# Inverse roots of a two-layer transformer kernel as one power instruction on GpSimd

## The chip, the cores and the metric

The kernel runs on one core of a Trainium2 chip. A core has TensorE (PE in the profile, its weight loads as PEld), VectorE (DVE), ScalarE (ACT), GpSimd (POOL) and SyncE (SP, which issues most DMAs), each with its own instruction stream; they meet by semaphores. The metric is the device time of one execution in microseconds, the median of three runs.

## The reference, cut to what matters

The input `x` is 8 x 256 tokens of 512 features, taken as 2048 tokens; the context is as many tokens of 256 features.

```python
def layernorm(x):  return (x - mean(x)) / sqrt(var(x) + 1e-5)
def rmsnorm(q, g): return q * rsqrt(mean(q*q) + 1e-5) * g      # over the 128 of a head

# first layer: cross attention (16 heads of 128, 8 key/value heads), then feed-forward
xn = layernorm(x)
q, k, v = xn @ Wq, ctx @ Wk, ctx @ Wv
x = x + softmax(q k^T / sqrt(128)) v @ Wo
x = x + feed_forward(layernorm(x))          # 512 -> 1536 -> 512, silu(gate) * up, scaled fp8 weights
# second layer: cross attention with normed queries and keys (16 heads of each), then experts
xn = layernorm(x)
q, k, v = rmsnorm(xn @ Wq, gq), rmsnorm(ctx @ Wk, gk), ctx @ Wv
x = x + softmax(q k^T / sqrt(128)) v @ Wo
x = x + experts(layernorm(x))               # 16 experts of width 256, the best 2 of sigmoid(logits)
```

An inverse root is needed four times for a layer norm (one number a token) and twice for an rms norm (one number a token and head).

## The kernel before, in words

All is in float32 precision: an operand of a product is split into a high and a low part of the faster type fp32r (`_hi`, `_lo`), and three products (high by high, high by low, low by high) make one. The tokens are 16 tiles of 128 (one a partition, `P` = 128, `NT` = 16), in four token groups of four tiles (`TG` = 4, `GT` = 512 tokens, `NG` = 4). The attention works through eight head groups of two heads (`HB` = 2, `NHG` = 8), and in each through the four token groups.

The program is five stages in a row: opening, first attention, feed-forward, second attention, experts (`moe_stage`). Each is a block in which every engine's program is written out by hand, in the order in which it is to run; a stage ends when all engines have reached its end. Work of a later stage (weights, normalised rows) is put into the stage before where room was found for it.

An inverse root is made by `rsqrt_steps` (L50): an integer seed from the bits of the number, then three Newton rounds of four small instructions. These are 13 instructions on [128, 4] or [128, 8], and each waits for the one before by a chain semaphore. They stand in these places:

- **The opening**, on VectorE: mean and variance of the first eight tiles (`bn_aggr`, then L241), the root, the shift `-mean * rstd` (L243). Then VectorE normalises tile 0, ScalarE tiles 1, 3, 5, 6 (L179) and GpSimd tiles 2, 4, 7 (L141). GpSimd's only earlier work there is the identity matrix `ident`; TensorE waits for it by `ident_made`.
- **The layer norms at the start and the end of an attention**, on GpSimd: `ln_group_factors` waits for VectorE's moments (`ln_mv`, L1379 or L1395), makes variance (L678), root and shift (L680, L683) and raises `ln_factors`. ScalarE waits for that and normalises rows (L1096), TensorE turns them (L884), and they become operands of the next stage. `late_factors(g)` does so for token group g in the last head group.
- **The second attention's rms norms**, on GpSimd: `norm_queries` waits for the sums of squares of the next token group's queries and for this group's exponentials, makes eight factors and raises `q_ready`. `norm_keys` waits for ScalarE's copy of the keys into `kn` (L1022), makes eight factors (variance L620, then the root), scales the keys by them in four instructions of 256 columns (L635) and raises `k_ready`; the first keys are scaled by VectorE instead. `first_query_factors` makes the first four query factors.
- **The last token group's layer norm before the experts**, on VectorE at the start of `moe_stage`: variance, root, shift; then VectorE normalises four rows (L2523), and ScalarE the four rows of the group before (L2390), whose factors were made in the attention.
- **The feed-forward layer's own**, on VectorE.

In each token group of the second attention VectorE takes the maxima of the scores and from them and the query factors the biases of the exponentials (L1308), ScalarE the exponentials (L1065), VectorE scales the probabilities by the reciprocal sums in pairs of instructions (L1333), TensorE turns them (L832), ScalarE and VectorE copy them out as high and low part (L1071, L1245), and TensorE multiplies them with the values (L733, as all split products). TensorE turns the scaled keys at L809. ScalarE copies the turned queries' high part at L1003 and the weighted values' high part at L1075. In `moe_stage` the routing's logits come from L2035, ScalarE's sigmoids are turned back at L2278.

`apart` raises a semaphore that nobody waits for; it separates an instruction from the wait before it.

## Time and profile before

| | |
|---|---|
| three runs | 2195.21, 2196.19 (median), 2196.66 us |
| profiled execution, span | 2195.1 us, 36404 instructions |
| TensorE (PE) busy | 2071.1 us, 94% |
| weight loads (PEld) | 1788.0 us, 81% |
| VectorE (DVE) | 1566.6 us, 71% |
| ScalarE (ACT) | 1253.3 us, 57% |
| GpSimd (POOL) | 574.9 us, 26% |

The span runs from the first to the last instruction of the profiled execution; the time of a run lies about 1 us above it. The busy shares are means over stages that differ: TensorE is at 90% or more in nearly all of the 40 slices of the page, and at about half in the first slice, in one at the change from the second attention to the experts, and in the last. A row of a timeline has the start in us, the duration of one (or the sum, where instructions of a kind stand together, x4), the engine, the line of the kernel, the operation, what it writes from what, with shapes, and in brackets how long the engine had been idle before and which instruction ended that. DVEq, POOLq and the like are an engine's sequencer.

### The profile page before, as it was taken

Reading aid. Unit: us, or ns where it says so; the run is one execution under the profiler, and the core shown is the slowest. Engines: PE = TensorE matmul, PEld = TensorE weight load, DVE = VectorE, ACT = ScalarE, POOL = GpSimd, SP = SyncE. Lnnn points to the kernel's source line nnn. Section 1 sums busy time; section 2 is a strip of 40 time slices with the busy share of each in tenths; the row PEclk is TensorE's granted clock in tenths of the full one; section 3 lists DMA queues with packets and bytes.
Section 4 is the critical chain, followed back from the end, with each engine's and each line's share of the span. In section 5 each row is a group of like instructions: output and inputs, shape, how many; then the busy total and the mean of one; then the engine's idle time right before and its main releaser. Section 6 shows DMA issues by size and latency. Waiting matters only on the chain. (4 is left out here: it accounts for less than half of the span.)

```text
span 2195.1 us, 36404 instructions
## 1 busy us (share of the span) xinstructions
PE 2071.1 (94%) x11594; PEld 1788.0 (81%) x11594; DVE 1566.6 (71%) x3714; ACT 1253.3 (57%) x3253; POOL 574.9 (26%) x1480
## 2 busy tenths in 40 slices
PE   5999999999999899999899999999999999599992
PEld 5888988888888778887788888888888887378882
DVE  6787677777779884444677777777777777767775
ACT  4555445455445533324776766677676666567771
POOL 2001001001001002223333434433343433145541
PEclk8999999999999999999999999999999999799996
DMA  7232122121211220002111111111111111278886
GB/s 249 82 99 89 63 85 92 62 89 63 90 63 49 73 77 1 1 1 77 49 58 49 62 63 57 48 57 48 57 62 72 48 40 39 87 269 290 290 275 257
DMA packets 78509, 202.10 MB, mean 92 GB/s; under 512 B 8689, under 2 KB 38409, under 8 KB 66209
## 3 DMA queue, kind: packets, MB, share of 16 engines
q1 hardware_dynamic: 68672, 179.37, 23.5%
q0 software_dynamic: 7520, 16.80, 2.2%
q10 hardware_dynamic: 2176, 4.19, 0.5%
q8 instruction: 72, 1.18, 0.2%
q14 instruction: 69, 0.56, 0.1%
HBM read 179.09 MB, written 29.10 MB: 95 GB/s over the span
## 5 line engine op out<-in xcount | busy, mean ns | idle before, releaser
L733 PE MATMUL bank<-l_wkv_hi,l_ctxT 128*128 128x512 f32 (+1 forms) x768 | 224.8, 364 | 9.0 <-PEq L79 6.9
L1245 DVE TENSOR_TENSOR l_pT_lo<-bank,l_pT_hi 128x512 fp32r<-128x512 f32 x256 | 175.2, 684 | 69.7 <-ACT l_pT_hi L1071 69.6
L1065 ACT ACTIVATE l_probs<-l_scored,l_nbias 128x256 f32<-128x256 f32 x256 | 128.4, 504 | 167.8 <-DVE l_nbias L1318 167.8
L733 PE MATMUL bank<-xnT_hi,l_wq_hi 128*128 128x512 f32 x512 | 208.7, 408 | 0.8 <-DVEq L1551 0.7
L733 PE MATMUL bank<-l_wo_hi,l_oT_hi 128*128 128x512 f32 x512 | 208.4, 407 | 0.7 <-DVE l_oT_lo L1245 0.7
L733 PE MATMUL bank<-l_wo_hi,l_oT_lo 128*128 128x512 f32 x512 | 200.6, 392 | 0.0
L733 PE MATMUL bank<-xnT_hi,l_wq_lo 128*128 128x512 f32 x512 | 200.3, 391 | 0.0
L733 PE MATMUL bank<-l_wo_lo,l_oT_hi 128*128 128x512 f32 x512 | 200.2, 391 | 0.0
L733 PE MATMUL bank<-xnT_lo,l_wq_hi 128*128 128x512 f32 x512 | 200.2, 391 | 0.0
L1071 ACT CAST l_pT_hi<-bank 128x512 fp32r<-128x512 f32 x256 | 150.8, 589 | 67.6 <-PE bank L832 67.6
L1333 DVE TENSOR_SCALAR l_probs<-l_probs,l_rden 128x256 f32<-128x256 f32 x512 | 181.3, 396 | 9.0
L1361 DVE TENSOR_TENSOR x_sb<-bank,x_sb 128x512 f32<-128x512 f32 x256 | 170.9, 683 | 7.8 <-PE bank L733 7.7
L832 PE MATMUL bank<-ident,l_probs 128*128 128x128 f32 x1024 | 156.5, 275 | 8.3 <-DVE l_probs L1333 8.3
L733 PEld LDWEIGHTS bank<-l_wkv_hi,l_ctxT 128*128 128x128 f32 x768 | 140.4, 194 | 28.9 <-issue 8.0
L1065 ACT ACTIVATE l_probs<-bank,l_nbias,l_rr 128x256 f32<-128x256 f32 x256 | 142.4, 565 | 34.2 <-DVE l_nbias L1308 33.6
L1983 PE MATMUL bank<-xnT_hi,ffn_w 128*128 128x512 f32 x384 | 151.5, 395 | 3.0 <-DVE ffn_w L1673 3.0
L733 PE MATMUL bank<-l_kT_hi,l_qT_hi 128*128 128x256 f32 x512 | 148.2, 289 | 5.7 <-DVE l_kT_lo L1245 3.1
L733 PE MATMUL bank<-l_pT_hi,l_v_hi 128*128 128x256 f32 x512 | 148.1, 289 | 5.3 <-DVE l_pT_lo L1245 4.3
L1983 PE MATMUL bank<-xnT_lo,ffn_w 128*128 128x512 f32 x384 | 149.6, 390 | 0.0
L733 PE MATMUL bank<-l_kT_lo,l_qT_hi 128*128 128x256 f32 x512 | 145.4, 284 | 0.0
L733 PE MATMUL bank<-l_kT_hi,l_qT_lo 128*128 128x256 f32 x512 | 145.4, 284 | 0.0
L733 PE MATMUL bank<-l_pT_lo,l_v_hi 128*128 128x256 f32 x512 | 145.1, 283 | 0.0
(305 smaller groups left out, 5738.0 us busy)
## 6 DMA issues: line engine op xcount, KB each, us to landing
l_ctxT<-ctx_split SPq DMA_DIRECT2D x63, 1024.0 KB, 4.8
moe_raw_gu<-in_L_ffn_gate_up_proj SPq DMA_DIRECT2D x31, 1024.0 KB
moe_raw_dn<-in_L_ffn_down_proj SPq DMA_DIRECT2D x31, 512.0 KB
l_raw_a<-in_L_xattn_Wq SPq DMA_DIRECT2D x16, 512.0 KB, 5.8
l_raw_a<-in_L_xattn_Wo SPq DMA_DIRECT2D x16, 512.0 KB, 5.6
x_sb<-in_x SPq DMA_DIRECT2D x4, 1024.0 KB, 9.1
l_v_next<-l_kn SPq DMA_DIRECT2D x16, 256.0 KB, 2.0
l_v_lo<-l_v_next SPq DMA_DIRECT2D x16, 256.0 KB, 2.6
```

What stands on the lines that cost most here:

```text
L733: mm = nc.tensor.matmul(out, a[x], b[y], start=(i == 0), stop=(i == n - 1))
L832: mm = nc.tensor.transpose(b_pt[:, S * s + P * t:S * s + P * (t + 1)], probs[u % 2][:, t, P * s:P * (s + 1)], k.ident[:, :])
L1065: ins = nc.scalar.activation(probs[u % 2][:, t, :], src, ACT.Exp, bias=nbias[:, i:i + 1], scale=scale, accum_out=rsum[:, i:i + 1])
L1071: nc.scalar.copy(pT[0][:, :, :].rearrange("p s q -> p (s q)"), b_pt[:, :]).then_inc(pT_hi, 1)
L1245: nc.vector.tensor_tensor(pair[1], src, pair[0].bitcast(F32), ALU.subtract).then_inc(done, 1)
L1333: ins = nc.vector.tensor_scalar(row, row, rden[:, 2 * u + t:2 * u + t + 1], None, ALU.mult)
L1361: nc.vector.tensor_tensor(row, b_q[t % 2][:, :], row, ALU.add).then_inc(y_added, 1)
L1983: mm = nc.tensor.matmul(out[r % 2][:, :], w[:, f, first + P * c:first + P * (c + 1)], part[:, c, at], start=(c == 0 and part is k.xnT_hi), ...
```

## The change

Outside of the feed-forward layer every inverse root becomes one GpSimd instruction, `tensor_tensor` with the power operation, of the variance and a tile `half` that holds -0.5 everywhere (`root_of`, `ROOT_STEPS` = 1). GpSimd fills `half` in the opening, ahead of the identity matrix. `rsqrt_steps` stays for the feed-forward layer.

- Opening: the root goes from VectorE to GpSimd. GpSimd waits for the variance (the chain at `CHAIN - 2`), VectorE waits for the root and makes the shift, as before.
- Attentions: GpSimd's chains are variance, power (and for a layer norm the two steps of the shift). The counts on the semaphores follow (`norm_steps`, `ln_steps`, and VectorE's waits on `k_chain` and `den_chain`).
- Experts: variance, root and shift of the last token group leave VectorE and `moe_stage`; GpSimd makes them with `late_factors(3)` at the end of its program in the second attention.

The diff, with hunks that only drop an unused scratch tile left out:

```diff
--- before.py
+++ after.py
@@ -61,6 +61,12 @@
 
 
 RSQRT_STEPS = 13
+ROOT_STEPS = 1
+
+
+def root_of(gp, y, v, half, step):
+
+    step(gp.tensor_tensor(y, v, half[:, 0:v.shape[1]], ALU.pow))
 
 
 def apart(k, eng):
@@ -92,7 +98,7 @@
         chain = k.ln0_chain
         mine = slice(0, TILES)
         DVE_TILES, ACT_TILES, POOL_TILES = (0, ), (1, 3, 5, 6), (2, 4, 7)
-        CHAIN = 2 * TILES + 1 + RSQRT_STEPS + 1
+        CHAIN = 2 * TILES + 1 + ROOT_STEPS + 1
         b_row = banks[4:8]
 
         def wait_normed(eng, t):
@@ -132,9 +138,12 @@
         def _(pool):
             gp = nc.gpsimd
             gp.memset(zero[:, :], 0.0).then_inc(ident_made, 1)
-            pool.wait_ge(ident_made, 1)
+            gp.memset(k.half[:, :], -0.5).then_inc(ident_made, 1)
+            pool.wait_ge(ident_made, 2)
             gp.affine_select(out=k.ident[:, :], in_=zero[:, :], compare_op=ALU.not_equal, fill=1.0, base=0,
                              pattern=[[-1, P]], channel_multiplier=1).then_inc(ident_made, 1)
+            pool.wait_ge(chain, CHAIN - 2)
+            gp.tensor_tensor(rstd[:, mine], var[:, mine], k.half[:, mine], ALU.pow).then_inc(chain, 1)
             pool.wait_ge(chain, CHAIN)
             for t in POOL_TILES:
                 apart(k, pool)
@@ -161,7 +170,7 @@
                     mm = nc.tensor.transpose(b_row[t % len(b_row)][:, P * c:P * (c + 1)], xn[t][:, P * c:P * (c + 1)], k.ident[:, :])
                 mm.then_inc(turned, 1)
 
-            pe.wait_ge(ident_made, 2)
+            pe.wait_ge(ident_made, 3)
             for g in range(2):
                 turn_c(g)
             for t in range(4):
@@ -239,7 +248,8 @@
             for t in range(TILES):
                 step(nc.vector.bn_aggr(mv[:, t, :], k.ln_stats[:, t, :]), t == TILES - 1)
             step(nc.vector.tensor_scalar(var[:, mine], mv[:, mine, 1], EPS, None, ALU.add))
-            rsqrt_steps(nc.vector, rstd[:, mine], tmp[:, mine], var[:, mine], step)
+            done[0] += 1
+            dve.wait_ge(chain, done[0])
             step(nc.vector.scalar_tensor_tensor(shift[:, mine], mv[:, mine, 0], -1.0, rstd[:, mine], ALU.mult, ALU.mult))
             for t in DVE_TILES:
                 nc.vector.tensor_scalar(xn[t][:, :], k.x_sb[:, t, :], mv[:, t, 0:1], rstd[:, t:t + 1],
@@ -605,7 +615,7 @@
             def weights_lo(w, raw, level, done):
                 start.weights_lo(pool, w, raw, level, done)
 
-            norm_steps = 1 + RSQRT_STEPS
+            norm_steps = 1 + ROOT_STEPS
 
             def factors(cols, chain, hg, g):
 
@@ -618,7 +628,7 @@
 
                 apart(k, pool)
                 step(gp.tensor_scalar(var[:, cols], sums[:, cols], 1.0 / HD, EPS, ALU.mult, ALU.add))
-                rsqrt_steps(gp, rr[:, cols], tmp[:, cols], var[:, cols], step, lambda: apart(k, pool))
+                root_of(gp, rr[:, cols], var[:, cols], k.half, step)
 
             def norm_keys(hg, g, first=False):
 
@@ -648,7 +658,7 @@
                 pool.wait_ge(qsum_out, 1)
                 apart(k, pool)
                 step(gp.tensor_scalar(var[:, cols], sums[:, cols], 1.0 / HD, EPS, ALU.mult, ALU.add))
-                rsqrt_steps(gp, rr[:, cols], tmp[:, cols], var[:, cols], step, lambda: apart(k, pool))
+                root_of(gp, rr[:, cols], var[:, cols], k.half, step)
 
             def norm_queries(hg, g):
 
@@ -657,14 +667,14 @@
                 factors(slice(nk, nk + nq), q_chain, hg, g - 1)
                 pool.sem_inc(q_ready, HB)
 
-            ln_steps = RSQRT_STEPS + 3
+            ln_steps = ROOT_STEPS + 3
 
             factors_before = [0]
 
             def ln_group_factors(tiles, aggregated):
 
                 at = slice(tiles[0], tiles[-1] + 1)
-                mean, var, rstd, tmp, shift = k.ln_mv[:, at, 0], *(a[:, at] for a in (k.ln_var, k.ln_rstd, k.ln_tmp, k.ln_shift))
+                mean, var, rstd, shift = k.ln_mv[:, at, 0], *(a[:, at] for a in (k.ln_var, k.ln_rstd, k.ln_shift))
                 done = [ln_steps * factors_before[0]]
                 factors_before[0] += 1
 
@@ -676,7 +686,7 @@
                 pool.wait_ge(ln_aggr, aggregated)
                 apart(k, pool)
                 step(gp.tensor_scalar(var, k.ln_mv[:, at, 1], 1.0, EPS, ALU.mult, ALU.add))
-                rsqrt_steps(gp, rstd, tmp, var, step, lambda: apart(k, pool))
+                root_of(gp, rstd, var, k.half, step)
                 step(gp.tensor_tensor(shift, mean, rstd, ALU.mult))
                 apart(k, pool)
                 step(gp.tensor_scalar(shift, shift, -1.0, 0.0, ALU.mult, ALU.add))
@@ -721,6 +731,8 @@
                         late_factors(2)
 
             iterations(pool, iteration)
+            if rms:
+                late_factors(3)
 
         @block.tensor
         def _(pe):
@@ -1380,7 +1392,7 @@
 
             def scale_first_keys():
 
-                dve.wait_ge(k_chain, 1 + RSQRT_STEPS)
+                dve.wait_ge(k_chain, 1 + ROOT_STEPS)
                 kn3 = kn[:, :, :].rearrange("p t (h d) -> p (t h) d", d=HD)
                 scale = rr[:, 0:nk].rearrange("p (a b) -> p a b", b=1).broadcast_to([P, nk, HD])
                 nc.vector.tensor_tensor(kn3, kn3, scale, ALU.mult).then_inc(k_ready, 1)
@@ -1442,7 +1454,7 @@
             if AHEAD:
                 turned_low(0, 1)
             if rms:
-                dve.wait_ge(den_chain, 1 + RSQRT_STEPS)
+                dve.wait_ge(den_chain, 1 + ROOT_STEPS)
             biases(0, 0, 0)
             if not rms:
                 denominators(0, 0, 0)
@@ -2120,8 +2132,8 @@
 
         assert nc.sbuf_base <= start.bottom
         block = st.enter_context(nc.Block())
-        factors_made, dve_normed, act_normed, turned, turned_hi, turned_lo = (
-            sem(n) for n in ("factors_made", "dve_normed", "act_normed", "turned", "turned_hi", "turned_lo"))
+        dve_normed, act_normed, turned, turned_hi, turned_lo = (
+            sem(n) for n in ("dve_normed", "act_normed", "turned", "turned_hi", "turned_lo"))
         logits_made, b_logits = start.logits_made, start.b_logits
         sigmoids_made, probs_turned, probs_copied, consts_made, route_chain, picked, ranked, rows_made, halves_made = (
             sem(n) for n in ("sigmoids_made", "probs_turned", "probs_copied", "consts_made", "route_chain", "picked", "ranked",
@@ -2515,10 +2527,6 @@
                 if wait:
                     dve.wait_ge(route_chain, done[0])
 
-            last = slice(LATE + TG, NT)
-            chain(v.tensor_scalar(var[:, last], mv[:, last, 1], EPS, None, ALU.add))
-            rsqrt_steps(v, rstd[:, last], tmp[:, last], var[:, last], chain)
-            v.scalar_tensor_tensor(shift[:, last], mv[:, last, 0], -1.0, rstd[:, last], ALU.mult, ALU.mult).then_inc(factors_made, 1)
             for t in DVE_TILES:
                 v.tensor_scalar(xn[:, t, :], k.x_sb[:, t, :], mv[:, t, 0:1], rstd[:, t:t + 1], ALU.subtract, ALU.mult).then_inc(dve_normed, 1)
             for t in range(LATE, NT):
@@ -2712,6 +2720,7 @@
         k.ln_mv = st.enter_context(nc.sbuf_tensor("ln_mv", [P, NT, 2], F32))
         k.ln_var, k.ln_rstd, k.ln_tmp, k.ln_shift = (
             st.enter_context(nc.sbuf_tensor(f"ln_{n}", [P, NT], F32)) for n in ("var", "rstd", "tmp", "shift"))
+        k.half = st.enter_context(nc.sbuf_tensor("half", [P, NT], F32))
         k.xn_stored = [k.sem(f"xn_stored{i}") for i in range(3)]
         xn_rows = nc.dram_tensor("xn_rows", (T, D), F32, kind="Internal").ap()
         rows_v = xn_rows.rearrange("(t p) d -> p t d", p=P)
```

## Rows read from the trace of the kernel before

**Rows 1.** Windows: each engine's busy us and instructions, granted clock, DMA.

```profile
1070.00:1830.00 760.00, 758.39 (x4405) 661.68 (x4405) 557.55 (x1203) 524.28 (x1644) 301.49 (x1045) 1.00 0.15 54
```

**Rows 2.** Timeline, opening: start us, us, engine, line, idle before and its releaser.

```profile
12.98 0.17 DVE L241 TENSOR_SCALAR ln_var<-ln_mv 128x8 f32<-128x8 f32 x1
...
15.83 0.17 DVE L243 SCALAR_TENSOR_TENSOR ln_shift<-ln_mv,ln_rstd 128x8 f32<-128x8 f32 x1
...
16.23 2.52 POOL L141 TENSOR_SCALAR xn<-x_sb,ln_rstd,ln_shift 128x512 f32<-128x512 f32 x3 [14.68 <-DVE ln_shift L243]
...
17.08 1.52 ACT L179 ACTIVATE xn<-x_sb,ln_shift,ln_rstd 128x512 f32<-128x512 f32 x2
```

**Rows 3.** Timeline, first attention's start: GpSimd, ScalarE, TensorE.

```profile
37.55 0.20 POOL L678 TENSOR_SCALAR ln_var<-ln_mv 128x8 f32<-128x8 f32 x1 [7.99 <-DVE ln_mv L1395]
...
37.95 0.20 POOL L54 TENSOR_SCALAR ln_rstd<-ln_var 128x8 int32<-128x8 int32 x1 [0.20 <-POOL ln_var L678]
...
41.94 0.20 POOL L680 TENSOR_TENSOR ln_shift<-ln_mv,ln_rstd 128x8 f32<-128x8 f32 x1
...
42.62 1.52 ACT L1096 ACTIVATE ffn_raw<-x_sb,ln_shift,ln_rstd 128x512 f32<-128x512 f32 x2 [3.44 <-POOLq L683]
...
44.04 0.56 ACT L1003 CAST l_qT_hi<-bank 128x512 fp32r<-128x512 f32 x1
...
43.48 1.36 PE L884 MATMUL bank<-ident,ffn_raw 128*128 128x128 f32 x8 [0.85 <-ACT ffn_raw L1096]
```

**Rows 4.** Timeline, first attention's end: GpSimd, ScalarE, VectorE, TensorE.

```profile
717.85 0.19 POOL L678 TENSOR_SCALAR ln_var<-ln_mv 128x4 f32<-128x4 f32 x1 [13.46 <-DVE ln_mv L1379]
...
724.17 1.52 ACT L1096 ACTIVATE l_raw_a<-x_sb,ln_shift,ln_rstd 128x512 f32<-128x512 f32 x2 [4.23 <-POOLq L683]
...
726.19 0.69 DVE L1245 TENSOR_TENSOR l_oT_lo<-bank,l_oT_hi 128x512 fp32r<-128x512 f32 x1 [1.73 <-ACT l_oT_hi L1075]
...
727.62 0.36 PE L733 MATMUL bank<-l_pT_hi,l_v_hi 128*128 128x256 f32 x1 [1.89 <-DVE l_pT_lo L1245]
```

**Rows 5.** Timeline, second attention's loop: groups from 1506 and 1532, one instruction at 1581.

```profile
1515.93 0.40 ACT L1022 COPY l_kn<-bank 128x256 f32<-128x256 f32 x1
...
1517.32 0.20 POOL L620 TENSOR_SCALAR l_var<-l_sums 128x8 f32<-128x8 f32 x1 [0.36 <-POOL l_rr L60]
...
1521.72 2.38 POOL L635 TENSOR_TENSOR l_kn<-l_kn,l_rr 128x256 f32<-128x256 f32 x4
...
1517.41 0.16 DVE L1308 SCALAR_TENSOR_TENSOR l_nbias<-l_mx,l_rr 128x2 f32<-128x2 f32 x1
...
1519.04 0.62 DVE L1333 TENSOR_SCALAR l_probs<-l_probs,l_rden 128x256 f32<-128x256 f32 x2
...
1523.12 1.13 DVE L1333 TENSOR_SCALAR l_probs<-l_probs,l_rden 128x256 f32<-128x256 f32 x2
...
1581.29 0.53 DVE L1308 SCALAR_TENSOR_TENSOR l_nbias<-l_mx,l_rr 128x2 f32<-128x2 f32 x1
...
1520.30 0.60 PE L832 MATMUL bank<-ident,l_probs 128*128 128x128 f32 x4
...
1524.31 0.42 PEld L832 LDWEIGHTS bank<-ident,l_probs 128*128 128x128 f32 x4 [0.15 <-DVE l_probs L1333]
...
1550.08 0.42 PEld L832 LDWEIGHTS bank<-ident,l_probs 128*128 128x128 f32 x4 [0.43 <-DVE l_probs L1333]
```

**Rows 6.** Timeline, from the second attention to the routing.

```profile
1871.16 0.38 DVE L1379 BATCH_NORM_AGGREGATE ln_mv<-ln_stats 128x2 f32<-128x6 f32 x4
...
1877.53 1.91 DVE L2523 TENSOR_SCALAR moe_xn<-x_sb,ln_mv,ln_rstd 128x512 f32<-128x512 f32 x4
...
1872.83 0.39 PE L2035 MATMUL bank<-xnT_lo,moe_gwT_hi 128*16 128x512 f32 x1
...
1873.53 2.93 ACT L2390 ACTIVATE moe_xn<-x_sb,ln_shift,ln_rstd 128x512 f32<-128x512 f32 x4 [11.42 <-PEq L386]
...
1880.42 0.61 PE L2278 MATMUL bank<-ident,moe_probT 16*128 16x16 f32 x4 [3.25 <-ACT moe_probT L2399]
```

More of the change, by code:

```diff
@@ L83, in opening_stage @@
         xn = [st.enter_context(nc.sbuf_tensor(f"xn_{j}", [P, D], F32)) for j in range(TILES)]
-        mv, var, rstd, tmp, shift = k.ln_mv, k.ln_var, k.ln_rstd, k.ln_tmp, k.ln_shift
+        mv, var, rstd, shift = k.ln_mv, k.ln_var, k.ln_rstd, k.ln_shift
         block = st.enter_context(nc.Block())
@@ L408, in attention_stage @@
             nk, nq = TG * nkv, TG * HB
-            sums, var, rr, tmp = (sb(n, [P, nk + nq]) for n in ("sums", "var", "rr", "tmp"))
+            sums, var, rr = (sb(n, [P, nk + nq]) for n in ("sums", "var", "rr"))
             gain_in = sb("gain_in", [P, 2])
@@ L2093, in moe_stage @@
         token_of, dest_of, expert_of = sb("token_of", [P, HALVES], I32), sb("dest_of", [P, HALVES], I32), sb("expert_of", [P, 2 * PAIRS], I32)
-        mv, var, rstd, tmp, shift = k.ln_mv, k.ln_var, k.ln_rstd, k.ln_tmp, k.ln_shift
+        mv, rstd, shift = k.ln_mv, k.ln_rstd, k.ln_shift
         warm = sb("warm", [P, 2])
```

## The prediction, before the changed kernel was run

> **What bounds the kernel now.** I read the windows first, to see which engine is full in which stretch, then the timelines of single stretches, looking for places where an engine stands idle behind an inverse root. In the second attention's loop TensorE is busy 758.4 of 760 us while VectorE has 558, ScalarE 524 and GpSimd 301 [rows 1]: shortening a GpSimd chain there is worth something only where it takes a stall away from TensorE. The start of each stage is different: there the engines hand work to each other and a root can set the pace. So I went to each of the places where a root is made.
>
> **The price of one root.** The old chain is 13 instructions: a seed and three rounds of four. A small instruction of GpSimd runs 0.20 us. A whole layer norm group (variance, 13 steps, two for the shift) goes from 37.55 to 42.62, when ScalarE takes over: 5.07 us. The seed starts at 37.95 and the shift at 41.94 [rows 3], so the 13 steps are 3.91 with the 0.08 between instructions off. After the change the same group is 5.07 - 3.91 = 1.16 us + X, where X is the power instruction.
>
> No row shows X. From below it is a multiply of the same shape, 0.20 us. From above it is the chain it replaces, 3.9 us. Between them: the key scaling, 128x256 in 0.595 us (four in 2.38 [rows 5]) against 0.20 for 8 columns, gives (0.595 - 0.20) / 248 = 1.6 ns a column. If a logarithm and an exponential are each worth one old chain, 26 arithmetic steps, X is 0.20 + 26 x 8 x 1.6 ns = 0.53 us for 8 columns and 0.37 for 4. Loops that don't fill the pipeline make it longer. I take 0.65 and 0.43 us, nearer to the lower end because the multiply's row shows that most of a small instruction is fixed cost. If the lanes were served one after another it would be 0.20 + 16 x 0.33 = 5.5 us.
>
> **Opening.** The variance ends at 13.15, the shift starts at 15.83 [rows 2]. Now the root crosses to GpSimd and back: a crossing is 0.23 (16.00 to 16.23), the way back some 0.1, so the shift starts at 13.15 + 0.23 + X + 0.1 = 14.1. That is 1.7 us earlier and worth nothing: the reader is to see that ScalarE starts to normalise at 17.08, with no idle time named, because it is still copying the context; the shift was there at 16.00. ScalarE is what the rest of this stage hangs on. The cover is 1.0 us; only with X above 2.7 does the root come too late. The extra memset of `half` lies beside a wait of 14.7 us [rows 2]. I book 0.
>
> **First attention, start.** ScalarE idles 3.44 us for the factors and normalises from 42.62; after it comes the copy of the second head's queries, at 44.04. TensorE had finished that product at 43.48 - 0.85 = 42.63 [rows 3]. With the factors at 37.55 + 1.16 + 0.65 = 39.4, two rows are normalised by 40.9 and the copy starts at 42.7, held by TensorE. Everything up to the first scores hangs on that copy: 44.04 - 42.71 = **-1.3 us**, in full for X up to 2.5.
>
> **First attention, end.** The late group starts at 717.85; ScalarE idles 4.23 us until 724.17, so it was free at 719.94. Behind that wait stand the copy of the weighted values and of the turned probabilities; VectorE waits 1.73 for them until 726.19, TensorE 1.89 until 727.62 [rows 4]. With the factors at 717.85 + 1.16 + 0.43 = 719.4 ScalarE goes on at once, its two copies end by 722.6, and VectorE goes on when it is done with its own work, at 726.19 - 1.73 = 724.46. TensorE's 1.89 falls to about 0.1: **-1.8 us**, in full for X up to 3.
>
> **Second attention, start.** Three chains in a row (keys, first queries, layer norm). VectorE is busy with statistics when the keys' factors come, TensorE's first scores come after the queries' factors, ScalarE's normalisation stands behind its own copies. Nobody waits for GpSimd there; 0.
>
> **Second attention, loop.** Of the 32 groups (8 head groups by 4 token groups) all but the first have their keys scaled by GpSimd: 31 groups each lose two chains of 3.9 us on an engine that nobody waits for. Yet there is an indirect effect. The reader is to look at the pair of probability scalings L1333: 0.62 us at 1519.04, but 1.13 at 1523.12 [rows 5]. The slow one lies under GpSimd's key scaling, 1521.72 to 1524.10, and ends 0.15 after it. TensorE waits for it: its weight load at 1524.31 carries 0.15 idle, and every fourth group it is 0.43, as at 1550.08 [rows 5]. TensorE is the bound, so that is lost time; with an estimated 0.07 by which the load before it is already late I count 0.22 in an ordinary group and 0.50 in each fourth.
> With one power instruction the key scaling moves. The keys' last copy ends at 1516.33; + 0.2 crossing + 0.28 variance = 1516.81, + X + 0.08: it runs 1517.54 to 1519.92. It now meets the scaling before, at 1519.04. Waiting first for the third and then for the fourth GpSimd instruction, that pair ends at 1519.92 + 0.16 = 1520.08 in place of 1519.66, 0.42 late. TensorE wants it at 1520.30 less its load [rows 5]: just hidden. VectorE carries the 0.42 on: the next pair starts at 1523.54, takes 0.62 free of GpSimd, and the load can go at 1524.22 where it went at 1524.31; in each fourth group at 1549.71 where it was 1550.08. That saves 0.09 in 22 groups and 0.37 in 8 (the first group has another order): 2.0 + 3.0 = **-5.0 us**. If the lateness were hidden wholly it would be 22 x 0.22 + 8 x 0.50 = -8.8.
>
> **Second attention's end and the routing.** ScalarE's wait before normalising late rows ends nothing that TensorE waits for. The last group's moments end at 1871.54 [rows 6]. After the change GpSimd makes their factors there: start 1871.7, + 1.1 + X = 1873.2. TensorE's last product ends at 1873.22 anyway, and the next stage starts at 1873.53. So no cost at X = 0.43, and X - 0.45 above it. What is gained is 4.0 us of VectorE, which now normalises from 1873.5 and not from 1877.53. That is not on the path: TensorE waits 3.25 us until 1880.42 for ScalarE's sigmoids [rows 6], which stand behind ScalarE's own four rows from 1873.53. 0.
>
> **The sum.** 0 - 1.3 - 1.8 + 0 - 5.0 + 0 = -8.1 us on a span of 2195.1: 2187.0. The three runs have their median at 2196.19, 1.1 above the span; with it 2188.1.
>
> **Rivals.**
> *Only the ends gain.* The lateness that the key scaling now causes one pair earlier eats what it no longer causes: 2196.2 - 3.1 = 2193. For it: by the same sums the saving per ordinary group is 0.09 us, and it is gone at X = 0.78. Against: each fourth group has more to give back.
> *The power instruction keeps VectorE off.* This ends on the other side. L1308 at 1517.41 reads two tensors of SBUF; at 1581.29 such a one took 0.53 in place of 0.16 [rows 5], with GpSimd at a weight split. The power instruction runs from 1516.81: with X above 0.6 it is in flight at 1517.41. At X = 1.5 L1308 ends at 1518.41 in place of 1517.57, the exponentials and the pair follow, the pair then meets the key scaling's last instruction and ends at 1520.9, TensorE stands 0.8 us less the 0.2 that it lost before, in all some 0.7 x 31 = 22 us, - 2 for the fourth groups, - 3 at the ends: 2213. It decides from X = 0.78 on, with 3 us for each further 0.1; from X about 0.95 the kernel is slower. Against it: at 1517.41 GpSimd's variance (1517.32 to 1517.52) is in flight, too, and L1308 takes its plain 0.16.
> The Trainium skill, SBUF — State Buffer, "Who interferes with whom", says of a VectorE instruction with two SBUF inputs, or in a two-port mode, that whichever engine issues first holds the shared pair for its whole instruction and the other blocks. By that rule this rival's arithmetic holds wherever X is above 0.6; the late pair at 1523.12 agrees with it, the plain 0.16 at 1517.41 does not show it.
> *A very slow power instruction.* With lanes in turn, 5.5 us, TensorE would stand some 5 us in each of 31 groups: 2340.
> The Trainium skill, GPSIMD Engine Reference, "Instruction dispatch", has about 6 us for the first call of newly loaded code. By it the opening's shift would come at 20 and not at 14, some 3 us behind ScalarE's readiness. No first instruction of a kind in this trace shows such a gap.
>
> **How the numbers follow.** A measurement of this kernel tells about 0.2% from no change, 4.4 us: faster is below 2191.8, slower above 2200.6. X up to 0.78, or a longer one that doesn't hold VectorE: 0.50, 2184 to 2191.8, faster. Only the ends gain, X of 0.78 to 0.95 or a collision as dear as before: 0.20, mostly within 0.2%. Keeping VectorE off: 0.23, slower. Very slow, or dear code loading: 0.07, slower. So 0.50, 0.20, 0.30. The likeliest case is 2188.1, its own range 2184 to 2192. For 8 in 10 the upper end reaches into the second rival to X about 1.3, 2196.2 - 5 + 17 = 2208; the lower end is the loop's stalls gone wholly, 2196.2 - 3.1 - 8.8 = 2184.
>
> **What would show it.** After: one GpSimd instruction of 0.4 to 0.7 us where 13 were; the first attention's scores 1.3 us earlier; no idle of ScalarE at its late rows; in the loop the key scaling under the third pair of L1333 and not the fourth, and the period of four groups some 0.6 us shorter; the routing starting as far behind TensorE's last product as now. Wrong: a root longer than 0.78 us, L1308 at more than 0.16 with the root in flight, or the third pair ending after 1520.2 on this scale, so that TensorE waits there.

## The result and the profile after

The changed kernel takes 2202.89 us (median of 5 runs, 2201.36 to 2203.88), the kernel before 2195.21 (5 runs, 2194.02 to 2196.66): ratio 1.0033, 95% interval 1.0022 to 1.0045. It is slower by some 7 us, where I had forecast 8 less. The profiled execution has a span of 2199.4 us.

The new instruction first. GpSimd's groups by line and shape (count, busy us, mean ns, idle time before):

```profile
L69 POOL TENSOR_TENSOR l_rr<-l_var,half 128x8 f32<-128x8 f32 x64 | 104.7, 1637 | 5.3
...
L69 POOL TENSOR_TENSOR ln_rstd<-ln_var,half 128x4 f32<-128x4 f32 x7 | 7.1, 1007 | 0.6
```

X is 1.64 us for 8 columns and 1.01 for 4: 0.158 us for each column and 0.38 beside. I had taken 0.65 and 0.43. It is still less than half of the chain's 3.9.

The timeline of the second attention's loop, the group that answers to [rows 5] (2.4 us later in this execution):

```profile
1518.93 0.20 POOL L630 TENSOR_SCALAR l_var<-l_sums 128x8 f32<-128x8 f32 x1 [1.94 <-ACT l_kn L1034]
1519.21 1.64 POOL L69 TENSOR_TENSOR l_rr<-l_var,half 128x8 f32<-128x8 f32 x1
1520.92 2.42 POOL L645 TENSOR_TENSOR l_kn<-l_kn,l_rr 128x256 f32<-128x256 f32 x4
...
1519.82 0.16 DVE L1320 SCALAR_TENSOR_TENSOR l_nbias<-l_mx,l_rr 128x2 f32<-128x2 f32 x1
...
1521.45 1.42 DVE L1345 TENSOR_SCALAR l_probs<-l_probs,l_rden 128x256 f32<-128x256 f32 x2
...
1526.17 0.61 DVE L1345 TENSOR_SCALAR l_probs<-l_probs,l_rden 128x256 f32<-128x256 f32 x2
...
1522.93 0.42 PEld L844 LDWEIGHTS bank<-ident,l_probs 128*128 128x128 f32 x4 [0.29 <-DVE l_probs L1345]
1526.84 0.42 PEld L844 LDWEIGHTS bank<-ident,l_probs 128*128 128x128 f32 x4
```

And the third pair's load in the kernel before:

```profile
1520.19 0.46 PEld L832 LDWEIGHTS bank<-ident,l_probs 128*128 128x128 f32 x4
```

The reader is to see three things. The key scaling (L645) has moved from the fourth pair of probability scalings to the third, as forecast. But it lies over the whole third pair, which takes 1.42 us in place of 0.62, and TensorE's load at 1522.93 waits 0.29 us for it, where the one at 1520.19 in the kernel before did not wait. And the bias (L1320, 0.16 us) is not touched by the power instruction, which is in flight from 1519.21 to 1520.85.

The first attention's start and end, and the way into the routing:

```profile
36.31 1.64 POOL L69 TENSOR_TENSOR ln_rstd<-ln_var,half 128x8 f32<-128x8 f32 x1
...
38.72 1.52 ACT L1108 ACTIVATE ffn_raw<-x_sb,ln_shift,ln_rstd 128x512 f32<-128x512 f32 x2 [1.16 <-POOLq L693]
...
41.16 0.58 ACT L1015 CAST l_qT_hi<-bank 128x512 fp32r<-128x512 f32 x1 [0.91 <-PE bank L745]
...
716.67 1.01 POOL L69 TENSOR_TENSOR ln_rstd<-ln_var,half 128x4 f32<-128x4 f32 x1
...
718.97 1.52 ACT L1108 ACTIVATE l_raw_a<-x_sb,ln_shift,ln_rstd 128x512 f32<-128x512 f32 x2 [0.51 <-POOLq L693]
...
724.29 0.19 PEld L745 LDWEIGHTS bank<-l_pT_hi,l_v_hi 128*128 128x128 f32 x1 [0.26 <-issue]
...
1876.58 0.39 PE L2047 MATMUL bank<-xnT_lo,moe_gwT_hi 128*16 128x512 f32 x1
...
1877.27 0.19 POOL L692 TENSOR_SCALAR ln_shift<-ln_shift 128x4 f32<-128x4 f32 x1 [0.20 <-POOL ln_shift L690]
...
1877.89 2.93 ACT L2402 ACTIVATE moe_xn<-x_sb,ln_shift,ln_rstd 128x512 f32<-128x512 f32 x4 [12.00 <-PEq L396]
...
1884.78 0.42 PE L2290 MATMUL bank<-ident,moe_probT 16*128 16x16 f32 x4 [3.25 <-ACT moe_probT L2411]
```

ScalarE waits 0.51 us where it waited 4.23 [rows 4], the queries' copy is held by TensorE and no more by the factors, and from ScalarE's first row of the routing to the turned probabilities it is 6.89 us as before [rows 6]. But that first row starts 0.92 us after TensorE's last product (1876.97 to 1877.89), where it was 0.31 (1873.22 to 1873.53): the last factors, ready at 1877.46, now come after that product.

What no row of mine had shown is in a stage whose code did not change. The groups of the feed-forward layer's products, changed kernel (mean ns last before the idle time):

```profile
L1995 PE MATMUL bank<-xnT_hi,ffn_w 128*128 128x512 f32 x384 | 153.3, 399 | 1.9 <-DVE ffn_w L1685 0.8
L1995 PE MATMUL bank<-xnT_lo,ffn_w 128*128 128x512 f32 x384 | 151.6, 395 | 0.0
```

Before they were 395 and 390 ns. Matmuls overlap, so their starts tell more: followed one by one in the two traces, such products (`xnT_hi` with `ffn_w`, then `xnT_lo` with `ffn_w`) start 227.5 ns apart before and 233.2 after, at the same granted clock of 1.00. That is the mean of the gaps below 260 ns; a longer one holds a stall. The forecasts below have 227.8 for the same. Where a stretch is bounded by TensorE that is time. I matched the weight loads of both traces by their number (11594 in each): the 1152 of the feed-forward layer's middle take 3.8 us longer after the change, 3632 of the first attention's loop 2.4 us longer. The same counting gives the period of the second attention's loop, four token groups: 102.13 us before, 102.68 after. These two numbers, stretch and period, are the measures of what follows.

### The profile page after: what moved, and what is told of

The parts are those of the page before. It is cut to its first block and busy times, and to the rows that moved or that the text cites. A ratio compares the mean times of both kernels' runs of the same rounds, so it can differ in the third digit from the quotient of the medians.

```text
span 2199.4 us, 34874 instructions
## 1 busy us (share of the span) xinstructions
PE 2075.8 (94%) x11594; PEld 1780.7 (81%) x11594; DVE 1565.1 (71%) x3686; ACT 1260.5 (57%) x3253; POOL 502.9 (23%) x622
## 5 line engine op out<-in xcount | busy, mean ns | idle before, releaser
L1345 DVE TENSOR_SCALAR l_probs<-l_probs,l_rden 128x256 f32<-128x256 f32 x512 | 188.1, 409 | 9.0
L1015 ACT CAST l_qT_hi<-bank 128x512 fp32r<-128x512 f32 x128 | 75.1, 587 | 127.2 <-PE bank L745 125.1
L745 PE MATMUL bank<-l_pT_hi,l_v_lo 128*128 128x256 f32 x512 | 144.9, 283 | 0.0
```

The source lines that it names most:

```text
L745: mm = nc.tensor.matmul(out, a[x], b[y], start=(i == 0), stop=(i == n - 1))
L1015: nc.scalar.copy(qT[h][0][:, :], b_q[h][:, :]).then_inc(q_hi, 1)
L1345: ins = nc.vector.tensor_scalar(row, row, rden[:, 2 * u + t:2 * u + t + 1], None, ALU.mult)
```

## The experiments

Theory 1: the tile `half` (64 bytes a partition) has pushed all tiles behind it to other addresses, and that slows TensorE. Theory 2: in the second attention the collision of the key scaling with the third pair costs more than the old one with the fourth. The rival to the first is that the pace differs by chance from one execution to another; to the second, that the power instruction keeps VectorE off.

**A tile that nobody uses.**

```diff
 # kernel before
+        k.pad = st.enter_context(nc.sbuf_tensor("pad", [P, NT], F32))   # where the change has half
```

> The kernel before, with one unused tile of 16 columns (64 bytes a partition) laid where the change lays its tile of -0.5, so that all tiles behind it lie 64 bytes further. Theory 1 (placement): in the changed kernel the products of 128x512 follow each other at 0.232 us in the feed-forward layer and 0.2317 in the first attention, where they stood at 0.227 and 0.2297 before, though their code is the same; the shift does it. Then this kernel shows the same slower pace, the feed-forward layer is 4 us longer, the first attention 2.4, and the whole is slower by 5 to 8 us (ratio 1.002 to 1.004). Rival: the pace differs from one execution to another and has nothing to do with the change; then this kernel takes the time of before within 2 us (ratio 0.999 to 1.001).

Ratio 1.0044 (1.0030 to 1.0058), feed-forward stretch +3.8 us, first attention +2.3: an unused tile does to the kernel before all that the change does to these two stages, and the whole becomes 9.7 us longer, more than by the change (7.2), with intervals that overlap. In the second attention's loop it does little: period 102.17.

**Every tile back in its place.**

```diff
 # changed kernel: half takes the scratch tile's place
-        k.ln_var, k.ln_rstd, k.ln_tmp, k.ln_shift = (... ("var", "rstd", "tmp", "shift"))
-        k.half = st.enter_context(nc.sbuf_tensor("half", [P, NT], F32))
+        k.ln_var, k.ln_rstd, k.half, k.ln_shift = (... ("ln_var", "ln_rstd", "half", "ln_shift"))
+        k.ln_tmp = k.ln_shift
-            sums, var, rr = (... ("sums", "var", "rr"))
+            sums, var, rr, _ = (... ("sums", "var", "rr", "spare"))
```

> The changed kernel, with the tile of -0.5 in the place of the scratch tile that the roots no longer need (the feed-forward layer's own root takes the shift's tile as scratch) and the second attention's scratch tile kept as an unused one, so that every other tile lies where it lay before. Placement theory: the pace goes back to 0.227 in the feed-forward layer, and the time falls from 2202.9 by 2.4 + 3.9 + about 1 to 2195.6 (ratio to before 1.000). Rival, pace by chance: as the changed kernel, ratio 1.003.

Ratio 0.9986 (0.9977 to 0.9995), 2192.73 us: faster than before, where I had expected equality. Stretch -0.05 us. Placement cost the change 0.0047 of 2196 us, 10.3 us, more than the 7.3 that I had added up from three stages. The period is 102.36, and 102.68 in the changed kernel: the loop has 2.5 us of it (7.75 periods), though the unused tile alone cost it next to nothing.

**The key scaling held back.**

```diff
 # changed kernel, norm_keys
+                apart(k, pool)
+                pool.wait_ge(p_normed, count(UN, 3, hg, g))
                 for i in range(0, nk, PIECE // HD):
```

> The changed kernel, with GpSimd's key scaling in the second attention made to wait until VectorE has scaled the third pair of probabilities. Collision theory: the third pair takes 0.62 us in place of 1.42, TensorE's turning load waits no longer (gap 0.48 to about 0.14), the fourth pair stays free; 31 groups save 0.34 each, 10 us: ratio to before 0.9985. Rival: the stall is not of this collision, or the scaling, 1.3 us later, meets the fourth pair or makes the turned keys late; then ratio 1.002 to 1.006.

Ratio 0.9985 (0.9976 to 0.9994), period 101.47: 1.21 us less than the changed kernel's. Timeline of this kernel, GpSimd and VectorE:

```profile
1515.37 0.62 DVE L1347 TENSOR_SCALAR l_probs<-l_probs,l_rden 128x256 f32<-128x256 f32 x2
1516.06 2.33 POOL L647 TENSOR_TENSOR l_kn<-l_kn,l_rr 128x256 f32<-128x256 f32 x4 [1.30 <-DVE l_probs L1347]
1517.21 0.62 DVE L1322 SCALAR_TENSOR_TENSOR l_nbias<-l_mx,l_rr 128x2 f32<-128x2 f32 x1
1519.74 0.62 DVE L1347 TENSOR_SCALAR l_probs<-l_probs,l_rden 128x256 f32<-128x256 f32 x2
```

The scaling fits between the two pairs, and both take 0.62 us. It now lies over a bias instead, which takes 0.62 us and not 0.16, and the period falls all the same. An engine that nobody waits for was made to start later, and the kernel became faster by 10 us.

**The old chain in the loop alone.**

```diff
 # changed kernel, factors() only (norm_steps, the wait on k_chain and the scratch tile with it)
-                root_of(gp, rr[:, cols], var[:, cols], k.half, step)
+                rsqrt_steps(gp, rr[:, cols], tmp[:, cols], var[:, cols], step, lambda: apart(k, pool))
```

> The changed kernel, with the old chain of 13 instructions for the factors of keys and queries in the second attention's loop alone (layer norms and first query factors keep the power instruction). Collision theory: the loop shows the pattern of before (fourth pair slow, third free), 0.19 us less in an ordinary group and 0.09 more in each fourth: 3.7 us off, ratio to before 1.0016. Rival, the loop is not what costs: ratio stays at 1.003.

Ratio 1.0023 (1.0014 to 1.0032), period 102.43, not 102.13: the direction is as forecast, the size some 2 us in place of 3.7. The unused tile alone gave a period of 102.17, so 0.26 us of it is not explained.

**Shifts by 128 and 32 bytes.**

```diff
 # kernel before, two runs
+        k.pad = st.enter_context(nc.sbuf_tensor("pad", [P, 2 * NT], F32))   # 128 bytes; [P, NT // 2] for 32
```

> The kernel before with one unused tile of 128 bytes a partition in the place where the earlier run had 64. Theory: what slows the products is that their operands no longer begin at a multiple of 128 bytes (the feed-forward weights begin at 116096 = 907 x 128, with the 64 byte tile at 116160). Then a shift by 128 costs nothing: feed-forward stretch as before, ratio 0.999 to 1.001. Rival: any shift against the tiles ahead (the turned activations stay where they are) costs the same: ratio 1.003 to 1.005, feed-forward +3.8 us.

> The same with 32 bytes. If 128 byte lines count, an operand that begins in the middle of one costs the same whether it is off by 32 or by 64: feed-forward stretch +3.8 us, ratio 1.003 to 1.005. If 32 bytes were the step that counts (all tiles still begin at multiples of 32), ratio 1.000, but then the 64 byte tile should have cost nothing either.

128 bytes: ratio 1.0031 (1.0020 to 1.0042), stretch +3.5. 32 bytes: 1.0052 (1.0038 to 1.0066), stretch +3.9. My theory of 128-byte lines fell: a shift by a whole line costs nearly the same. These two shifts also cost where the 64 bytes did little: the loop's period is 102.40 with 32 bytes and 102.38 with 128, and the experts' products from 1930 to 2150 us take 2.7 and 1.7 us longer (0.6 with 64). But the pace by pairs of operands pointed on. Mean ns between the starts of products of 512 columns, gaps below 260 ns (the last column is the next experiment):

| product, then the next | before | +32 B | +64 B | +128 B | 64 B ahead of all |
|---|---|---|---|---|---|
| xnT_hi with ffn_w, then xnT_lo with ffn_w | 227.5 | 232.5 | 233.3 | 235.7 | 227.6 |
| xnT_lo with ffn_w, then xnT_hi with ffn_w | 227.5 | 234.0 | 233.3 | 229.9 | 227.6 |
| xnT_hi with l_wq_hi, then xnT_lo with l_wq_hi | 229.3 | 233.3 | 233.5 | 232.2 | 230.6 |
| moe_w_dn_lo with xnT_hi, then moe_w_dn_hi with xnT_lo | 226.7 | 234.6 | 231.2 | 232.1 | 226.7 |
| l_wo_hi with l_oT_hi, then l_wo_lo with l_oT_hi | 228.4 | 228.1 | 227.3 | 228.1 | 230.1 |
| ffn_w with ffn_fz_hi, then ffn_w with ffn_fz_lo | 226.8 | 228.8 | 229.1 | 229.2 | 226.8 |
| ffn_w with ffn_fz_lo, then ffn_w with ffn_fz_hi | 226.8 | 230.1 | 231.1 | 229.6 | 226.8 |

In the first four rows one operand moved (weights) and one did not (`xnT`, laid ahead of the new tile), and all are slower. In the last three both moved. The row of `l_wo` is no slower behind `xnT` (with the tile ahead of all it is, by 1.7 ns); those of `ffn_w` with `ffn_fz` are, by 2.0 to 4.3 ns.

**The same tile ahead of all others.**

```diff
 # kernel before
+        k.pad = st.enter_context(nc.sbuf_tensor("pad", [P, NT], F32))
         k.x_sb = st.enter_context(nc.sbuf_tensor("x_sb", [P, NT, D], F32))
```

> The kernel before with the unused 64 bytes ahead of all tiles, so that the turned activations move as well and every tile lies to every other as before, except for the few that are counted from the end of the memory. The runs so far show a slower pace where a product takes one operand that moved and one that did not (turned activations with feed-forward or query weights: 227.8 to 233.3 ns), with shifts of 32, 64 and 128 bytes. Theory, the distance between the two operands counts: these products stay at 227.8 and the feed-forward stretch as long as before, ratio 0.999 to 1.001. Rival, the address of the moving operand itself counts: 233, feed-forward stretch +3.8 us, ratio 1.003 or more.

Ratio 1.0002 (0.9993 to 1.0011), stretch -0.03 us, period 102.15. The same shift of 64 bytes costs nothing when `xnT` takes part in it. So it is not a tile's own place that counts, but how the tiles that moved lie to those that stayed. That it is the distance between a product's own two operands is not shown: `ffn_w` and `ffn_fz` moved together behind `xnT` and got slower, and move together here and do not. The groups of these products, first with the tile ahead of all, then (second fence) behind `xnT`:

```profile
L1983 PE MATMUL bank<-xnT_hi,ffn_w 128*128 128x512 f32 x384 | 151.6, 395 | 2.9 <-DVE ffn_w L1673 2.9
L1983 PE MATMUL bank<-xnT_lo,ffn_w 128*128 128x512 f32 x384 | 149.6, 390 | 0.0
```

```profile
L1983 PE MATMUL bank<-xnT_hi,ffn_w 128*128 128x512 f32 x384 | 153.3, 399 | 1.8 <-DVE ffn_w L1673 0.8
L1983 PE MATMUL bank<-xnT_lo,ffn_w 128*128 128x512 f32 x384 | 151.6, 395 | 0.0
```

**The layer norms alone.** Every tile in its place, and the old chain in the loop.

> The changed kernel with every tile where it lay before, and the old chain of 13 instructions for the factors of keys and queries in the second attention's loop: what is left of the change are the layer norms (opening, attention starts and ends, the routing's last group). By my prediction's terms the ends give 3.1 us; the loop then has the period of before, 102.14 us for four groups, where the unshifted power version has 102.36, so it is some 1.7 us faster than that one: ratio 0.998. Rival: the loop's period differs for another reason than the chains; then it stays at 102.36 and the ratio at 0.9986.

Ratio 0.9981 (0.9972 to 0.9990), period 102.21. The layer norms by one instruction give 4.2 us, and some 4.8 if the loop's 0.08 a period over the kernel before is set aside. The loop itself, with the power instruction and no shift, has 102.36: 0.15 more a period, 1.2 us over its 7.75 periods, and 0.23 or 1.8 us more than in the kernel before. The two ratios (0.9986 and 0.9981) say 1.1, less than their intervals can tell; the period rests on one trace each.

**Both repairs.**

> Both repairs together: every tile where it lay before, and the key scaling held back until the third pair is scaled. If the two costs are separate, they add: the period falls from 102.36 by the 1.2 us that the hold-back gave in the shifted kernel to 101.15, and the time to 2192.7 - 9.3 = 2183.4, ratio 0.994. Rival: they overlap (a stall hides behind a slower pace), then 0.996 to 0.9985.

Ratio 0.9943 (0.9929 to 0.9957), 2184.36 us, period 101.19. The two costs are separate and add up within the intervals: the hold-back gives 1.21 a period with the shift and 1.17 without.

**More work, less time.**

```diff
 # changed kernel, tiles in their places, factors()
+                if chain is k_chain:
+                    gp.tensor_tensor(spare[:, cols], var[:, cols], k.half[:, 0:nk], ALU.pow)
                 root_of(gp, rr[:, cols], var[:, cols], k.half, step)
```

> The changed kernel with every tile where it lay before, and the power instruction for the keys' factors issued twice (once into an unused tile), so that this step takes GpSimd 3.3 us and not 1.6. Collision theory: the key scaling then begins 1.7 us later, after the third pair of probabilities and before the fourth, and more work makes the kernel faster: period of four groups 101.2 us in place of 102.36, ratio 0.9943 as with the hold-back. If the power instruction itself kept VectorE off, its second copy would cost: the small bias instruction takes more than 0.16 us and the period is above 102.4, ratio above 0.9986.

Ratio 0.9940 (0.9927 to 0.9954), period 101.19. Its timeline:

```profile
1506.48 1.64 POOL L632 TENSOR_TENSOR l_spare<-l_var,half 128x8 f32<-128x8 f32 x1
1508.08 1.64 POOL L69 TENSOR_TENSOR l_rr<-l_var,half 128x8 f32<-128x8 f32 x1
1509.79 2.33 POOL L647 TENSOR_TENSOR l_kn<-l_kn,l_rr 128x256 f32<-128x256 f32 x4
...
1507.10 0.16 DVE L1322 SCALAR_TENSOR_TENSOR l_nbias<-l_mx,l_rr 128x2 f32<-128x2 f32 x1
...
1508.73 0.62 DVE L1347 TENSOR_SCALAR l_probs<-l_probs,l_rden 128x256 f32<-128x256 f32 x2
...
1510.57 0.42 DVE L1322 SCALAR_TENSOR_TENSOR l_nbias<-l_mx,l_rr 128x2 f32<-128x2 f32 x1
```

A power instruction that is thrown away makes the kernel 10 us faster (0.9940 and 0.9986) than the same without it, since the key scaling starts after the third pair. The pair at 1508.73 lies wholly under a power instruction and takes its plain 0.62; the bias takes 0.16 under the power instruction and 0.42 under the key scaling. It holds in the whole loop: each of the 31 biases that start under a power instruction takes 0.16, and each of the 62 instructions of such pairs 0.35 to 0.36, as those free of GpSimd. So it is the scaling that holds VectorE up, not the root.

**The two moves undone.** Both repairs, but the opening's root and the routing's last factors back on VectorE as 13 steps.

```diff
-            gp.tensor_tensor(rstd[:, mine], var[:, mine], k.half[:, mine], ALU.pow).then_inc(chain, 1)   # opening, GpSimd
+            rsqrt_steps(nc.vector, rstd[:, mine], shift[:, mine], var[:, mine], step)                    # opening, VectorE
-                late_factors(3)
+            rsqrt_steps(v, rstd[:, last], shift[:, last], var[:, last], chain)                           # experts, VectorE
```

> The version with both repairs (0.9943), with the opening's root back on VectorE as 13 steps and the routing's last group's factors back on VectorE at the start of the experts. My prediction books both moves at 0: ratio 0.993 to 0.9955. If the opening's earlier shift or VectorE's earlier rows in the routing were worth something, it is slower by up to 1 + 4 us: 0.9965.

Ratio 0.9947 (0.9933 to 0.9961): the two moves are worth nothing that can be told from 0.9943, by a measurement that leaves some 3 us open on either side. The traces tell the routing's move more closely: the weight loads that stand at 1872 and 1875 us in the kernel before lie 0.6 to 0.8 us further apart in each kernel with `late_factors(3)`, and as before (0.0) in this one.

**Three lines.** The scratch tile kept and the key scaling held back, as above, and `half` ahead of all tiles:

```diff
+        k.half = st.enter_context(nc.sbuf_tensor("half", [P, NT], F32))
         k.x_sb = st.enter_context(nc.sbuf_tensor("x_sb", [P, NT, D], F32))
 ...
-        k.half = st.enter_context(nc.sbuf_tensor("half", [P, NT], F32))
```

> The changed kernel as it stands, with three lines different: the tile of -0.5 laid ahead of all other tiles, the second attention's scratch tile kept as an unused one, and the key scaling held back until the third pair is scaled. All tiles lie 64 bytes further than before, but as before to each other. If it is the distance between operands that counts, the feed-forward products go at 227.8 ns and the time is that of the version with both repairs, ratio 0.9943. If the changed kernel has another cost that comes with moving tiles at all, ratio 0.997 to 1.000.

Ratio 0.9958 (0.9945 to 0.9972), 2187.05 us: between the two forecasts, and nearer to 0.9943, whose interval it overlaps; a cost of up to some 3 us is not excluded. Its trace shows none: stretch -0.01 us, products at 227.6 ns, period 101.19 as in the version with both repairs, and from 60 us on no stage is more than 1 us longer than there.

## Why the prediction was wrong, step by step

- **The new tile.** The step that failed most was one that I did not take: I booked `half` at its memset and let its 64 bytes weigh nothing. They put every tile behind it at another distance from `xnT`, and products with one operand on either side slow down by 2 to 3% (227.5 to 233.2 ns). With what else slows, that is 10.3 us of 2196 (1.0033 less 0.9986), more than the 8.1 that I forecast as gain, so it turns the sign by itself.
- **The price of one root.** Mis-sized: X was 1.64 and 1.01 us, not 0.65 and 0.43. The 0.158 us for a column is a hundred times the 1.6 ns that I read off a multiply, where I had allowed for 26 steps of that price.
- **Second attention, loop.** The mechanism held (the key scaling leaves the fourth pair and meets the third), its size and sign did not: -5.0 forecast, +1.1 to +1.2 measured against the old chain in the same places and +1.8 by the period against the kernel before (102.36 and 102.13). With X = 1.64 in my own line the scaling runs from 1518.53 to 1520.91 and covers both instructions of the pair at 1519.04, not the end of it. I had counted 0.42 of lateness; full cover is 0.80 (1.42 less 0.62), and the half microsecond of slack behind that pair no longer hides it. The old collision covered part of a pair, 1.13 us [rows 5]: a pair wholly covered must be dearer, and that could have been read. Two of my three signs of being wrong came: the root above 0.78 us, and a third pair that ends after 1520.2 (1522.87 here, 1520.46 on that scale).
- **First attention, start and end.** -1.3 and -1.8, with X in full cover up to 2.5 and 3: right in kind. At the start the weight loads that stand at 38 and 44 us in the kernel before are 1.2 to 1.3 us closer in all nine kernels with the power instruction, and 0.1 to 0.2 us further apart in the four with an unused tile alone. The whole stretch can't be read so closely, since the granted clock from 25 to 60 us was 0.76 before and with 128 bytes, and between 0.80 and 0.90 in the others. At the end the same weight loads come 2.5 us closer in each of the nine, against 1.8. Together with the rest outside the second attention's old chain the runs give -4.2 (interval -6.1 to -2.2) against my -3.1.
- **Opening and routing.** Booked at 0. The kernel with both moves undone can't be told from the one with them, and the routing's 0.6 us in the traces is my own "X - 0.45 above it" at X = 1.01: a cost that came from the mis-sized X, and too small for the times to show. In the opening I had misadded the limit: the root comes too late for ScalarE with X above some 3.4 (0.65 + 1.7 + 1.0), not 2.7; X stayed below both. The second attention's start was booked at 0, too, and no run tests it by itself.
- **The rivals.** "Only the ends gain" came nearest for the change without its shift: it had 2193, and 2192.7 was measured. That is luck in part: the ends gave about 1 us more and the loop cost about 1 us, where it had nothing. "The power instruction keeps VectorE off" had the sign, and my range for 8 in 10 (2184 to 2208) held 2202.9 by its help alone, by a mechanism that did not occur: with X = 1.64 it should have cost over 20 us.

The three differences of the ratios (ends -4.2, loop +1.1, placement +10.3) give +7.2 us by construction, since each starts where the one before ends; their sum proves nothing. The traces give one that could have failed, in us from the kernel before to the changed one: first attention's start -1.2, its loop +2.4, its end -2.6, feed-forward layer +3.9, second attention's loop 7.75 x 0.55 = +4.3, routing +0.6, experts +0.7. That is +8.1, where the times say 7.2 (4.8 to 9.9). It is an estimate: it leaves out that the changed kernel's first 100 us are 2.7 us shorter beside, at a granted clock of 0.90 and not 0.76 from 25 to 60 us.

The Trainium skill, SBUF — State Buffer, "Who interferes with whom", has a GpSimd instruction that reads SBUF and a VectorE instruction with two SBUF inputs, or in a two-port mode, exclude each other for the whole of the one that came first. The key scaling agrees with it (a pair of 1.42 in place of 0.62, a bias of 0.62 in place of 0.16), the power instruction does not: it is in flight for 1.64 us and reads two tiles, and the bias, with two SBUF inputs, takes 0.16 under it and the pair 0.62. The measurement decides. The Trainium skill, GPSIMD Engine Reference, "Instruction dispatch", has about 6 us for a first call of newly loaded code; no run here shows that: the first power instruction starts 0.09 us after its operand is written and takes 1.68:

```profile
12.90 0.17 DVE L250 TENSOR_SCALAR ln_var<-ln_mv 128x8 f32<-128x8 f32 x1
13.16 1.68 POOL L146 TENSOR_TENSOR ln_rstd<-ln_var,half 128x8 f32<-128x8 f32 x1 [11.56 <-DVE ln_var L250]
```

**What stays open.** Why the place of moved tiles against unmoved ones counts, between which tiles, and which shifts are good: 0 is, and 32, 64 and 128 bytes are not, in this layout; larger ones were not run. A rival is untested: that what slows a product is another engine's access to a tile that stayed (`xnT`, `x_sb`), and not the product's own other operand. That other operand pairs move by one to four nanoseconds, `ffn_w` with `ffn_fz` above all, was not followed up. And the old chain in the loop has a period of 102.43 with the shift and 102.21 without, where the kernel before has 102.17 and 102.13; these 0.1 to 0.3 us have no cause that I could show. The shifts by 32 and 128 bytes alone make 0.25 to 0.27, so the loop's pace, too, hangs on placement.

## What to carry to other kernels

A new tile need not be free, however small: lay it ahead of all others or into the place of one that goes, and compare the pace of products in a stage that was not touched before reading anything else. A faster engine off the critical path moves its later work under other work: after shortening a chain, look at what its next large instruction now lies under, and if that is VectorE's, hold it back with a wait; here this was worth 9 to 10 us, and with the tiles in their places the whole change becomes 0.9943 in place of 1.0033. The price of an operation that no trace shows should have a range in which a column can cost far more than a multiply's, here a hundred times, and each term should be worked out at both ends of it.

## What the runs showed of the hardware

- Float32 power on GpSimd: 1.64 us for 128x8, 1.01 for 128x4, so 0.158 us a column and 0.38 beside, without holding up VectorE. A multiply of 128x8 takes 0.20.
- Four multiplies of 128x256 on GpSimd (2.3 to 2.4 us) over two VectorE scalings of 128x256 make these 1.42 us in place of 0.62, and a bias of 128x2 0.42 to 0.63 in place of 0.16.
- Products of 512 columns start 227.5 ns apart or 232.5 to 235.7 at the same granted clock of 1.00, by how the tiles of their operands lie to others in SBUF: 32, 64 or 128 bytes between `xnT` and the weights slow them, 64 bytes ahead of both do not (227.6).
